# One f32 TanH per step in place of an f16/remainder pair: the softmax scores come from an f32 matmul

## The reference, cut to what matters

```python
def step(carry, tgt):
    s, c, alpha = carry
    f = lax.conv_general_dilated(alpha, conv_w, (1,), 'SAME', ...)
    e = jnp.einsum('a,bta->bt', va, jnp.tanh(enc_proj + (s @ Wa_s.T)[:, None, :]
                                             + jnp.einsum('bft,af->bta', f, Wa_f) + ba))
    e = jnp.where(mask, e, jnp.float32(-1e+30))
    alpha_new = jax.nn.softmax(e, axis=1)[:, None, :]
    g = jnp.einsum('bt,btd->bd', alpha_new[:, 0], hbatch)
    y = jnp.tanh(g @ L_gy_w.T + L_gy_b + s @ L_sy.T) @ L_yy_w.T + L_yy_b
    rec = tgt @ L_ys.T + s @ L_ss.T + g @ L_gs_w.T + L_gs_b
    ig, fg, cg, og = jnp.split(rec, 4, axis=1)
    c_next = _sig(fg) * c + _sig(ig) * jnp.tanh(cg)
    s_next = _sig(og) * jnp.tanh(c_next)
    return ((s_next, c_next, alpha_new), y)
```

## Time and profile before

| | |
|---|---|
| Median of 3 executions | 1775.03 us (1773.21 to 1776.44) |
| Span of the profiled execution | 1777.0 us |
| PE busy | 1506.0 us (85%), 15683 matmul records |
| PE's weight loads (PEld) busy | 1022.2 us (58%) |
| DVE busy | 919.2 us (52%) |
| ACT busy | 528.9 us (30%) |
| POOL busy | 387.5 us (22%) |

### The profile page before, as it was taken

One profiled execution on the slowest core, in us unless ns is written; L12 is line 12 of the kernel. 1 busy time (PEld: TensorE's weight loads), 2 busy tenths in 40 slices (PEclk: granted clock), 3 DMA queues, 4 the chain that ended last, 5 costly groups with the idle time before them and its releaser, 6 DMA issues.

```text
span 1777.0 us, 43152 instructions
## 1 busy us (share of the span) xinstructions
PE 1506.0 (85%) x15683; PEld 1022.2 (58%) x15683; DVE 919.2 (52%) x4293; ACT 528.9 (30%) x2023; POOL 387.5 (22%) x1030
## 2 busy tenths in 40 slices
PE   6547999999888888888888888888888888887999
PEld 3334454544666666666666666666666666664443
DVE  4996643331555555555555555555555555553422
ACT  1342231221333333333333333333333333331211
POOL 3344321220000222222222222222222222222211
PEclk7658999999555555555555555555555555555999
DMA  8330000001200000000000000000000000000000
GB/s 326 141 115 11 1 1 0 1 1 52 77 0 0 0 0 0 0 0 0 0 0 0 0 0 0 0 0 0 0 0 0 0 0 0 0 0 1 1 24 25
DMA packets 17363, 34.51 MB, mean 19 GB/s; under 512 B 7476, under 2 KB 8675, under 8 KB 17332
## 3 DMA queue, kind: packets, MB, share of 16 engines
q1 hardware_dynamic: 17332, 34.10, 5.3%
HBM read 32.00 MB, written 2.10 MB: 19 GB/s over the span
## 4 chain that ended last, share of the span: by engine, by line
PE 62%; DVE 25%; issue 6%; ACT 5%; POOL 1%; DVEq 1%; SPq 1%; DMA 0%; POOLq 0%; ACTq 0%
PE bank L1243 18%; PE bank L1073 11%; PE bank L1193 6%; PE bank L1088 6%; PE bank L1221 5%; ACT eh L960 4%; DVE interT L746 4%; PE bank L1199 4%; DVE krep L764 3%; PE bank L1213 3%; DVE rinv L755 3%; DVE rs L743 2%; DVE g L760 2%; PE bank L1231 2%; DVE gat L771 2%
## 5 line engine op out<-in xcount | busy, mean ns | idle before, releaser
L1243 PE MATMUL bank<-krep,uh 128*128 128x128 f32 x1024 | 313.1, 461 | 23.6
L1243 PEld LDWEIGHTS bank<-krep,uh 128*128 128x128 f32 x1024 | 237.4, 320 | 92.4 <-DVE krep L764 92.4
L493 POOL TENSOR_TENSOR sscale<-ex,rinv 128x8 f32 x256 | 51.3, 200 | 667.6 <-DVE rinv L755 667.6
L1221 PE MATMUL bank<-eh,krep 128*128 128x4 f16 x2048 | 95.3, 168 | 92.5 <-ACT eh L960 92.5
L764 DVE TENSOR_TENSOR krep<-inv,ahn 128x128 f32<-128x128 f32 x512 | 162.2, 356 | 0.0
L1073 PE MATMUL bank<-xT,wbig 128*128 128x512 f16 x672 | 157.2, 386 | 3.7 <-DVE xT L591 3.7
L743 DVE TENSOR_TENSOR rs<-bank,rin 128x8 f32<-128x8 f32 x256 | 42.8, 167 | 198.1 <-PE bank L1199 198.1
L1221 PEld LDWEIGHTS bank<-eh,krep 128*128 128x128 f16 x2048 | 74.1, 105 | 114.0 <-ACT eh L960 114.0
L963 ACT ACTIVATE xs<-gat 64x8 f32<-64x8 f32 x256 | 53.4, 208 | 288.7 <-DVE gat L771 288.7
L955 ACT ACTIVATE interT<-bank 128x128 f16<-128x128 f32 x256 | 71.2, 278 | 216.9 <-PE bank L1193 216.9
L1181 PE MATMUL bank<-enc,identb 128*128 128x128 bf16 x771 | 128.4, 303 | 0.0
(11 more groups left out here) (201 smaller groups left out, 3044.5 us busy)
## 6 DMA issues: line engine op xcount, KB each, us to landing
wbig<-d_gate_qT SPq DMA_DIRECT2D x4, 896.0 KB, 10.1
wbig<-d_up_qT SPq DMA_DIRECT2D x4, 896.0 KB, 20.7
wbig<-d_down_qT SPq DMA_DIRECT2D x1, 3584.0 KB, 30.5
d_out<-x_sb SPq DMA_DIRECT2D x8, 256.0 KB, 2.0
sscale<-d_gate_sT SPq DMA_DIRECT2D x2, 896.0 KB, 8.6
interT<-d_gate_sT SPq DMA_DIRECT2D x2, 896.0 KB, 14.9
sscale<-d_up_sT SPq DMA_DIRECT2D x2, 896.0 KB, 4.2
interT<-d_up_sT SPq DMA_DIRECT2D x2, 896.0 KB, 4.3
```

The lines of the kernel that those rows point to most:

```text
L1221: ins = mm(bank[4][:, 4 * gp:4 * gp + 4], hg2[:, j, h, gp * P:(gp + 1) * P], e[:, 4 * h:4 * h + 4], start=(first and gp == 0 and j == 0 an ...
L1243: mm(bank[1 - par][:, 0:P], uh[:, h, :], qv[:, h, :, :], start=False, stop=False, skip_group_check=True)
```

## The change

The f16 TanH, the remainder, its matmul and `vae2` are gone. ACT writes the TanH once, in f32. The eight matmuls for the maximum read the upper 16 bits of each f32 value as bf16, so their moving data has a step of 4 bytes between elements. The scores come from one f32 matmul, with `th` (128x128 f32) as weights and `vae` (128x8 f32) as moving data.

```diff
-        vae2 = sb("vae2", [P, 2, 2 * B], F16)
...
-        th_hi = interT[:, 6, P:P + P // 2].bitcast(F16)
-        th_lo = interT[:, 6, 2 * P:2 * P + P // 2].bitcast(F16)
+        th_top = th.bitcast(BF16).rearrange("p (n two) -> p two n", two=2)[:, 1, :]
...
-            in_halves(vae2[:], vae[:].rearrange("p h b -> p (h b)"))
...
-                    dve.wait_ge(s["th_full"], l + 1)
-                    nc.vector.tensor_tensor(th_lo, th, th_hi, ALU.subtract).then_inc(s["th_lo_ready"], 1)
...
-                    nc.scalar.activation(th_hi, bank[par][:, 0:P], ACT.Tanh).then_inc(s["th_s"], 1)
                     nc.scalar.activation(th, bank[par][:, 0:P], ACT.Tanh).then_inc(s["th_full"], 1)
...
-            pe.wait_ge(s["part_ready"], 5)
+            pe.wait_ge(s["part_ready"], 4)
...
-                    pe.wait_ge(s["th_s"], l + 1)
+                    pe.wait_ge(s["th_full"], l + 1)
                     for b in range(B):
                         for h in range(2):
-                            last = mm(bank[2][b * TH:(b + 1) * TH, h * TH:(h + 1) * TH], vah[:, h, :], th_hi[:, b * TH:(b + 1) * TH],
+                            last = mm(bank[2][b * TH:(b + 1) * TH, h * TH:(h + 1) * TH], vah[:, h, :], th_top[:, b * TH:(b + 1) * TH],
                                       start=False, stop=True, skip_group_check=True)
                     last.then_inc(s["eb_done"], 1)
 
-                    for j in range(2):
-                        mm(bank[3][:, 0:8], th_hi, vae2[:, j, :], start=False, stop=False, skip_group_check=True)
-                    pe.wait_ge(s["th_lo_ready"], l + 1)
-                    mm(bank[3][:, 0:8], th_lo, vae2[:, 0, :], start=False, stop=True, skip_group_check=True).then_inc(s["et_done"], 1)
+                    mm(bank[3][:, 0:8], th, vae[:].rearrange("p h b -> p (h b)"), start=False, stop=True, skip_group_check=True).then_inc(s["et_done"], 1)
```

More of the change, by code:

```diff
@@ L264, in build @@
             vbd_zero setup_v setup_mm setup_cp mask_ready scale_ready
-            pre_done th_s th_full th_lo_ready eb_done et_done mx_ready eh_ready ex_ready el_ready sum_done ah_done hg_done rinv_ready ahn_ready
+            pre_done th_full eb_done et_done mx_ready eh_ready ex_ready el_ready sum_done ah_done hg_done rinv_ready ahn_ready
             prod_ready g_ready q0_ready q1_ready kept tg_ready ab_ready c_ready tc_ready s_ready sh_ready sl_ready sp_done
```

## The result

Four executions of the changed kernel took 1799.98 to 1809.45 us, with a median of 1801.24; the kernel before had 1774.78 beside them. The ratio is 1.0152, with a 95% interval of 1.0122 to 1.0183. The forecast was 1799.3 us, in a range of 1790 to 1814. The span of the profiled execution is 1798.2 us, for which 1801.3 was forecast, and its time 1799.98. In every execution here of which both are on record, the time is 1.8 to 1.9 us longer than the span. By that the profiled execution of the kernel before, with its span of 1777.0, took some 1779 us and was a long one beside the median of 1775; differences between spans have to be read with this in mind.

What follows compares the result with a forecast made beforehand. The recurrence loop bounds the kernel, with the remainder path setting each exponential's start. The f32 matmul delays it 0.095 us over 256 steps, 24.3 us, added to the median 1775.03 for 1799.3 us; range 1790 to 1814.

Steps and rivals of the forecast that it cites:

- Start of the f32 weights: On PE in each step: f32 weights wait for matmuls of another width, loading 0.07 to 0.08 us before those end.
- Length of 0.60: The f32 scores matmul in each step takes 0.60 us, bounds 0.58 to 0.61, mostly loading of f32 weights.
- One TanH in place of two: On ACT in each step: dropping the second TanH is worth 0, as ACT then waited for the third scores matmul.
- the 4-byte step: Small matmuls reading every other 16 bits cost 0; at worst 0.05 us a step, 13 us in all.
- The 0 for the setup: Before the loop, two DVE operations of 0.15 and 0.17 us go, worth 0; uncovered, 0.3 us once.
- The maximum's bound: If DVE's maximum alone decided, the exponential would start 0.17 us sooner a step, at most 43.5 us saved.
- rival A: The f32 scores pair is as cheap as an f16 pair, 0.21 us; maximum decides, 1731.5 us; 5 in 100.
- The sum: Over the loop: exponential 0.095 us later in 256 steps, 24.3 us, giving 1799.3 us against the median.
- Rival B: On PE, f32 weights load while the small matmuls still run; exponential moves by -0.01 us, 1772.5 us; 4 in 100.
- Rival D: The clock rises to 2.4 GHz in the loop; a step loses about 0.7 us, time near 1600; 4 in 100.

Runs made afterwards that it cites:

- the quarters: Changed kernel with its f32 matmul cut in four, each with weights 32 columns wide: 1753.14 us (ratio 0.9875 against the kernel before).
- the halves: Changed kernel with its f32 matmul cut in two, each with weights 64 columns wide: 1753.62 us (ratio 0.9878 against the kernel before).
- the run with the f32 matmul ahead: Changed kernel with the f32 matmul issued before the eight small matmuls on PE: 1889.67 us (ratio 1.0644 against the kernel before).
- the second matmul: Changed kernel with its f32 matmul issued twice: 1909.23 us (ratio 1.0754 against the kernel before).
- the run with the f32 matmul alone: Kernel before with both TanHs kept, the remainder and its three f16 matmuls replaced by the f32 matmul: 1803.85 us (ratio 1.0163).

## Why the prediction was right, point by point

- **Start of the f32 weights** (0.07 before the small matmuls' end, taken from L1211 and L1126): right, 904.44 against 904.51. That it is the change of width was a guess from two places; the quarters, the halves and the run with the f32 matmul ahead show it. So this term came right on a guess that the later runs bore out.
- **Length of 0.60**, by the line through 16 and 34 columns: measured 0.60. That most of it is loading is shown by the second matmul (0.424 a step) and by the quarters (0.30).
- **One TanH in place of two, 0; the 4-byte step, 0:** right for this change, since the step of the run with the f32 matmul alone is the same to 0.001 us. For a kernel that keeps the remainder it is wrong: there the second TanH stands in the way by some 0.04 a step, 11 of the 14 us that the loop gets shorter. The 0 for the setup no run takes apart; its bound, 0.3 us once, is too small to be seen.
- **The maximum's bound** (exponential 0.17 sooner, 43.5 us, "the most this change can save"): wrong in size. The runs in which the maximum decides win 0.090 a step, 23 us. I had put both handovers at 0.04, the gap from L1213 to ACT. They are 0.07 from the small matmuls to DVE and 0.09 from DVE to ACT. The forecast does not rest on it, since the f32 matmul ended 0.23 after the maximum; rival A's 1731.5 does, and would have been near 1755.
- **The sum:** 0.095 x 256 = 24.3 forecast, 23.6 measured in the loop, 26.5 between the medians, 21.2 between the spans, where the kernel before had its long execution. The interval of the ratio is 22 to 32 us, so the 3 us between loop and medians can't be told from the scatter of executions.
- **Rival A** (f32 as cheap as f16) is refuted for weights of full width: 0.60 against 0.21. In quarters f32 takes 0.30, which would have been enough. The rule of the Trainium skill, "TensorE: Matmul & The Clock Gate", section "LDWEIGHTS (loading the stationary operand)", that a load depends on its columns alone, does not hold in these traces once the type is f32. Two loads of 128 columns take 0.50 us in f32 (L1203), 0.13 in f16 (L1211 of the earlier trace rows).
- **Rival B** (weights pulled ahead) did not occur here. With equal widths it does, as the quarters show, whose f32 loads start 0.21 before the small matmuls end. There the trace agrees with the Trainium skill, "TensorE: Matmul & The Clock Gate", section "Step-by-step: what each phase is for", by which weight loads are pulled ahead of running matmuls.
- **Rival D** (clock): 0.50 in the loop, as before, though PE was busy for 1014 of 1159 us.
